# A graph-network layer on one core: the W2 sum leaves GpSimd, and two matmul rounds take up what is no longer summed

## What is computed

```python
xs, xv = _split(x, 64, 32)          # of node_features[col], col = dst
es, ev = _split(e, 8, 8)
s1 = einsum('ea,eb,abc->ec', xs, es, W1) * c1
s2 = einsum('eai,ebi,abc->ec', xv, ev, W2) * c2
out_s = (s1 + s2) * inv_sqrt2
v1 = einsum('ea,ebi,abc->eci', xs, ev, W3) * c3
v2 = einsum('eai,eb,abc->eci', xv, es, W4) * c4
out_v = (v1 + v2) * inv_sqrt2
messages = concatenate([out_s, out_v]) @ Wm + bm
agg = segment_sum(messages, row)    # row = src
upd = concatenate([node_features, agg]) @ Wu + bu
out = layernorm(x + node_features + upd)
```

## Time and profile before

| | |
|---|---|
| median of 3 runs | 2093.25 us (2091.78 to 2100.47) |
| the profiled execution | 2112.58 us |
| its span | 2110.8 us |
| TensorE matmul busy | 1648.6 us, 78% of the span |
| VectorE busy | 1647.6 us, 78% |
| GpSimd busy | 1333.6 us, 63% |
| ScalarE busy | 911.8 us, 43% |
| TensorE clock granted, mean | 0.916 |

### The profile page before, as it was taken

How to read it: one execution, slowest core, us unless ns; L and a number is a source line. 1 busy time by engine, 2 the same in 40 slices (tenths; PEclk the granted TensorE clock), 3 DMA queues, 4 the chain that set the end, 5 groups by cost and what they waited for, 6 DMA issues and landing times.

```text
span 2110.8 us, 37127 instructions
## 1 busy us (share of the span) xinstructions
PE 1648.6 (78%) x11180; PEld 987.9 (47%) x11180; DVE 1647.6 (78%) x1976; ACT 911.8 (43%) x1770; POOL 1333.6 (63%) x1082
## 2 busy tenths in 40 slices
PE   2535878787877887888787787878877878589995
PEld 1213444444444444444444444444444444388884
DVE  3545787878788788888888887878878888289996
ACT  1212444444444444444344343434443444267776
POOL 3206777777777777777777777777777777512221
PEclk9767998999999999989999999989989999899998
DMA  7996777777777777777777777777777776499996
GB/s 259 378 374 177 199 214 208 225 201 215 207 209 215 204 226 206 208 225 200 217 210 206 217 206 219 209 210 209 209 208 208 210 209 153 70 381 391 392 389 226
DMA packets 192108, 490.83 MB, mean 233 GB/s; under 512 B 51924, under 2 KB 104212, under 8 KB 166994
## 3 DMA queue, kind: packets, MB, share of 16 engines
q1 hardware_dynamic: 108994, 381.38, 51.6%
q0 software_dynamic: 83088, 109.13, 24.5%
HBM read 393.52 MB, written 96.88 MB: 232 GB/s over the span
## 4 chain that ended last, share of the span: by engine, by line
issue 23%; POOL 20%; DMA 18%; PE 16%; DVE 11%; ACT 3%; another core or an unknown queue 3%; SPq 2%; DVEq 1%; POOLq 1%; ACTq 0%
DMA agg<-summed,row_idx 13%; POOL agg L330 9%; POOL xg L305 7%; POOL prod L315 5%; DVE prod L521 4%; DMA agg<-start_rows 4%; PE ps L665 4%; PE ps L660 3%; PE ps L717 2%; DVE stats L609 2%; PE ps L648 2%; ACT prod L465 2%; PE ps L718 1%; PE ps L719 1%
## 5 line engine op out<-in xcount | busy, mean ns | idle before, releaser
L665 PE MATMUL ps<-prod,w_sb 128*32 128x512 f32 x2352 | 624.5, 665 | 335.5 <-POOL prod L315 246.3
L330 POOL DMA_INDIRECT agg<-summed,row_idx x392 | 623.8, 1591 | 399.9 <-DMA agg<-summed,row_idx 245.9
L521 DVE TENSOR_TENSOR prod<-ps,e_sb 128x2048 f32<-128x2048 f32 x294 | 662.4, 2285 | 187.3 <-PE ps L648 125.6
L305 POOL DMA_INDIRECT xg<-in_x_rows,dst_sb x392 | 399.3, 1019 | 146.3 <-issue 101.9
L315 POOL TENSOR_TENSOR prod<-prod 128x512 f32<-128x512 f32 x196 | 360.7, 1840 | 18.0 <-DVE prod L521 18.0
L529 DVE TENSOR_TENSOR prod<-ps,e_sb 128x3072 f32<-128x3072 f32 x98 | 328.0, 3347 | 0.2 <-PE ps L656 0.2
L509 DVE TENSOR_TENSOR prod<-ps,e_sb 128x2048 f32<-128x2048 f32 x98 | 223.9, 2285 | 102.8 <-PE ps L665 65.4
L432 ACT ACTIVATE summed<-ps 128x644 f32<-128x644 f32 x98 | 69.3, 707 | 541.2 <-PE ps L720 460.3
L665 PEld LDWEIGHTS ps<-prod,w_sb 128*32 128x32 f32 x2352 | 105.9, 112 | 378.9 <-POOL prod L315 267.3
L660 PE MATMUL ps<-prod,w_sb 128*32 128x512 f32 x1176 | 214.4, 617 | 0.0
L762 PE MATMUL ps<-wux_a,prod 128*128 128x160 f32 x784 | 181.0, 313 | 30.8 <-DVE prod L591 27.2
(11 more groups left out here) (62 smaller groups left out, 2358.1 us busy)
## 6 DMA issues: line engine op xcount, KB each, us to landing
e_sb<-in_e_rep SPq DMA_DIRECT2D x98, 1536.0 KB
e_sb<-in_e_rep SPq DMA_DIRECT2D x98, 1024.0 KB
agg<-start_rows SPq DMA_DIRECT2D x50, 640.0 KB, 5.1
prod<-in_x_t SPq DMA_DIRECT2D x98, 320.0 KB, 5.8
prod<-agg SPq DMA_DIRECT2D x97, 320.0 KB, 5.5
out<-prod POOLq DMA_DIRECT2D x97, 320.0 KB, 5.4
row_sb<-in_src_row SPq DMA_DIRECT2D x98, 256.0 KB
xg<-in_x_rows,dst_sb POOLq DMA_INDIRECT x392
```

Source lines behind the costliest of these rows:

```text
L305: nc.gpsimd.indirect_dma_start(xg[g[1] % 2][:, q, :], None, x_rows, bass.IndirectOffsetOnAxis(dst_sb[g[1]][:, q:q + 1].bitcast(U32), 0)).t ...
L330: nc.gpsimd.indirect_dma_start(agg, bass.IndirectOffsetOnAxis(row_idx[g[1]][:, q:q + 1].bitcast(U32), 0), summed[g[1]][:, q // 2, q % 2 * ...
L521: nc.vector.tensor_tensor(prod[g[1] % 2][:, 4 + 4 * i:8 + 4 * i, :].rearrange("p (a b) e -> p a b e", b=2), ps[:, t_bank(g, 1 + i), :].uns ...
L665: return nc.tensor.matmul(ps[32 * quarter:32 * quarter + 32, S_BANK, :], w[:, 32 * half:32 * half + 32], prod[g[1] % 2][:, tile, :], start ...
```

## The change

GpSimd's adds go away. VectorE makes one add of 1024 columns in place of two of 512: tiles 6 and 7 receive 10 and 11, after `times_xv(g, 1)`. Tiles 14 and 15 are no longer added to anything, and W2 contracts them itself: the scalar rounds take eight tiles (0 to 3, 6, 7, 14, 15). A new function `round_rest` follows `round_y` with four matmuls: one in quarter 0, one in quarter 1 and two in quarter 3. The count of rounds for a group is eight. GpSimd's slot becomes two gathers, two scatters, two gathers, two scatters. VectorE makes both steps of `rows` ahead of `times_xv(s, 0)`. TensorE transposes the first third of the next group's vectors after `round_w2`, no longer at the slot's end.

```diff
@@ -20,7 +20,7 @@
 ET = 10
 NPROD = 22
 USES = 6
-ROUNDS = 6
+ROUNDS = 8
 XW = 224
 MW = D + 1
 SET_ROWS = 8
@@ -307,14 +306,6 @@
                     bass.IndirectOffsetOnAxis(dst_sb[g[1]][:, q:q + 1].bitcast(U32), 0)
                 ).then_inc(x_gathered[g[1]], 16)
 
-            def add_parts(g, step):
-                pool.wait_ge(multiplied, number(g) * USES + 3 + step)
-                if step:
-                    pool.wait_ge(parts_added_pool, number(g) * 2 + 1)
-                total = prod[g[1] % 2][:, 6, :]
-                nc.gpsimd.tensor_tensor(total, total, prod[g[1] % 2][:, 10 + 4 * step, :],
-                                        ALU.add).then_inc(parts_added_pool, 1)
-
             def scatter(g, q):
                 if q == 0:
                     pool.wait_ge(summed_copied, number(g) + 1)
@@ -333,19 +324,13 @@
 
             def slot(s):
                 live = lambda d: not isinstance(s[0], int) or 0 <= number(s) + d < n_groups
-                for q in range(TILES):
+                for pair in range(2):
                     if live(2):
-                        gather(shift(s, 2), q)
-                if live(-3):
-                    scatter(shift(s, -3), 0)
-                    scatter(shift(s, -3), 1)
-                if live(0):
-                    add_parts(s, 0)
-                if live(-3):
-                    scatter(shift(s, -3), 2)
-                    scatter(shift(s, -3), 3)
-                if live(0):
-                    add_parts(s, 1)
+                        gather(shift(s, 2), 2 * pair)
+                        gather(shift(s, 2), 2 * pair + 1)
+                    if live(-3):
+                        scatter(shift(s, -3), 2 * pair)
+                        scatter(shift(s, -3), 2 * pair + 1)
 
             run_slots(pool, slot, -2, n_groups + 3, 8, (n_groups - 2) // M1 * M1)
@@ -531,13 +516,10 @@
                                         e_sb[g[1] % 2][:, 4:ET, :].rearrange("p (i f) e -> p f i e", f=2),
                                         ALU.mult).then_inc(multiplied, 2)
 
-            def add_parts(g, step):
-                dve.wait_ge(multiplied, number(g) * USES + 3 + step)
-                if step:
-                    dve.wait_ge(parts_added_dve, number(g) * 2 + 1)
-                total = prod[g[1] % 2][:, 7, :]
-                nc.vector.tensor_tensor(total, total, prod[g[1] % 2][:, 11 + 4 * step, :],
-                                        ALU.add).then_inc(parts_added_dve, 1)
+            def add_parts(g):
+                dve.wait_ge(multiplied, number(g) * USES + 3)
+                total = prod[g[1] % 2][:, 6:8, :]
+                nc.vector.tensor_tensor(total, total, prod[g[1] % 2][:, 10:12, :], ALU.add).then_inc(parts_added, 1)
 
             def rows(g, step):
                 n = number(g)
@@ -566,16 +548,13 @@
                     times_xs(s)
                 if live(-3):
                     rows(shift(s, -3), 0)
+                    rows(shift(s, -3), 1)
                 if live(0):
                     times_xv(s, 0)
-                if live(-3):
-                    rows(shift(s, -3), 1)
-                if live(0):
                     times_xv(s, 1)
+                    add_parts(s)
                     times_xv(s, 2)
-                    add_parts(s, 0)
                     times_y(s)
-                    add_parts(s, 1)
 
             run_slots(dve, slot, 0, n_groups + 3, 8, n_groups // M1 * M1)
@@ -661,7 +640,9 @@
                                         start=start, stop=stop)
 
             def scalars(g, quarter, k, half, start=False, stop=False):
-                tile, w = (k, w1_sb[:, k, :]) if k < 4 else (6 + k - 4, w2_sb[:, k - 4, :])
+
+                tile = (0, 1, 2, 3, 6, 7, 14, 15)[k]
+                w = w1_sb[:, k, :] if k < 4 else w2_sb[:, k % 2, :]
                 return nc.tensor.matmul(ps[32 * quarter:32 * quarter + 32, S_BANK, :], w[:, 32 * half:32 * half + 32],
                                         prod[g[1] % 2][:, tile, :], start=start, stop=stop)
@@ -683,10 +664,9 @@
                 scalars(g, 3, 1 + f, 0).then_inc(rounds, 1)
 
             def round_w2(g):
-                pe.wait_ge(parts_added_pool, number(g) * 2 + 2)
-                pe.wait_ge(parts_added_dve, number(g) * 2 + 2)
+                pe.wait_ge(parts_added, number(g) + 1)
                 for quarter in range(3):
-                    scalars(g, quarter, 3 + quarter, 1, stop=True)
+                    scalars(g, quarter, 3 + quarter, 1, stop=quarter == 2)
                 scalars(g, 3, 3, 0).then_inc(rounds, 1)
 
             def round_y(g, f):
@@ -694,7 +674,13 @@
                     pe.wait_ge(multiplied, number(g) * USES + 6)
                 for i in range(3):
                     vectors(g, i, 16 + 3 * f + i, sum_sb[:, :], stop=f == 1)
-                scalars(g, 3, 4 + f, 0, stop=f == 1).then_inc(rounds, 1)
+                scalars(g, 3, 4 + f, 0).then_inc(rounds, 1)
+
+            def round_rest(g):
+                scalars(g, 0, 6, 1, stop=True)
+                scalars(g, 1, 7, 1, stop=True)
+                scalars(g, 3, 6, 0).then_inc(rounds, 1)
+                scalars(g, 3, 7, 0, stop=True).then_inc(rounds, 1)
 
             def messages(g):
                 pe.wait_ge(S_copied, number(g) + 1)
@@ -740,13 +726,14 @@
                     transpose_xs(after)
                 if live(-1):
                     round_w2(before)
+                if live(1):
+                    transpose_xv(after, 0)
                 if live(-2):
                     sum_same(two_before)
                 if live(-1):
                     round_y(before, 0)
                     round_y(before, 1)
-                if live(1):
-                    transpose_xv(after, 0)
+                    round_rest(before)
 
             run_slots(pe, slot, -1, n_groups + 2, 8, (n_groups - 1) // M1 * M1)
```

More of the change, by code:

```diff
@@ L157, in build @@
         nodes_out = [sem(f"nodes_out{b}") for b in range(M2)]
-        parts_added_pool = sem("parts_added_pool")
         pool_passed = sem("pool_passed")
@@ L185, in build @@
         multiplied = sem("multiplied")
-        parts_added_dve = sem("parts_added_dve")
+        parts_added = sem("parts_added")
         idx_step = sem("idx_step")
```

## The result

The changed kernel takes **1966.97 us** (median of 4 runs, 1963.45 to 1973.67), the kernel before 2096.86 beside it (4 runs). The ratio is **0.937**, with a 95% interval of 0.9339 to 0.9401. I had predicted 2016 us and a range of 1890 to 2130, so the time lies within the range, and the gain is 130 us where I forecast 77. The profile shows that this is right for a reason that is partly wrong. All ratios count the executions within 1.5% of a kernel's fastest alone, which matters most for the changed kernel with late transposes, where it leaves out two of four executions and later four of six.

The account below looks back on a forecast made before the run. GpSimd's chain of 17.35 us was taken to bound the 17.50 us slot. TensorE's loop of 14.90 plus 1.80 of hold gives 16.7: 74 us over 92 slots, plus 5, less 2, off 2093 is 2016 us, range 1890 to 2130.

Parts of the forecast that it names:

- 5.14: GpSimd's wait in us from second to third scatter, including landing; used for both waits, giving a 14.1 us slot.
- GpSimd stays the bound: Rival: two open landing waits, each grown from 5.14 to 6.8 us, slot 17.5, 2090 us; chance 0.10.
- The moved gathers: GpSimd's third and fourth gathers, 2.7 us, go into the first landing wait: 4.6 us against 5.14.
- 14.90 us plus the hold: TensorE's loop from S copy to S copy after the change, claimed to set the slot.
- the hold: Time from the end of TensorE's last round's record to the S copy; taken as 1.80 us, cause unknown.
- Paid in full, 1.77: TensorE's round_rest: four more steps, 1.77 us, claimed to lie wholly on the path that sets the slot.
- My first rival: No hold: 0.07 us left, slot 15.0 us, 1860 us in all; chance 0.24.
- 16.7 forecast: Main case's slot in us: TensorE's loop of 14.90 plus 1.80 of hold, 0.8 less than before; chance 0.46.
- the slot with 4.08: A slot of the kernel before with edge loads, where the hold lasted 4.08 us, until the scatter pair ended.
- forecast 1.21: VectorE's single add of 1024 columns, claimed to take 1.21 us.
- 13.6 us of own work: VectorE's own work in a slot after the change, below TensorE's loop.
- forecast 5 and 2: 5 us gained before the sixth group's times_xs; 2 us lost at the end to the last group's extra rounds.

Follow-up runs that it names:

- changed kernel with late transposes: Changed kernel, TensorE's transposes for times_xv 0 put back to the end of its slot: 1910.21 us, ratio 0.8996; repeated, 1985.34 us, ratio 0.9254.
- six-round kernel with the new order: Changed kernel without round_rest, both 1024-column adds on VectorE, two gathers then two scatters, twice, on GpSimd: 1936.38 us, ratio 0.9197.
- light loads: Changed kernel with each group's second edge load cut from 1536 KB to 256 KB after the first two groups (output differs): 1850.69 us, ratio 0.8794.
- changed with the old order: Changed kernel with GpSimd put back to four gathers, then four scatters: 2113.31 us, ratio 1.0019.
- early transposes: Kernel before, with only TensorE's transposes for times_xv 0 of the next group moved ahead of sum_same: 2109.49 us, ratio 1.0022.

## Why the prediction was right and where it was wrong

**GpSimd: the step that failed.** "With 5.14 for both waits the slot is 14.1; GpSimd stops being the bound." It stayed the bound. The 5.14 was the first pair's figure, and I gave it to both pairs. The first pair's own mean in the kernel before is not far off: 5.28 over the 75 slots from 300 to 1600 us. But that mean has two parts. In 43 slots the second scatter starts 3.4 to 3.5 us after the issue of a 1536 KB load, and the next pair comes 5.95 later; in 32 it starts 6.0 to 7.9 after, and the next pair comes 4.38 later. One slot of the first kind, from GpSimd's timeline of the kernel before:

```profile
305.50 1.57 POOL L330 DMA_INDIRECT agg<-summed,row_idx  x1 [0.31 <-issue]
...
312.40 1.56 POOL L330 DMA_INDIRECT agg<-summed,row_idx  x1 [4.00 <-DMA agg<-summed,row_idx]
```

The second pair's second scatter started 2.4 to 7.1 us ahead of a load, and the pair after it came only 8.4 later, behind an add and four gathers, with no wait. So no row of the kernel before gave the landing time that the change laid open.

In the changed kernel I counted from the second scatter of a pair to the next pair, over the 164 pairs from 300 to 1600 us. The 82 whose second scatter starts from 4.5 us before to 1.5 us after the issue of a 1536 KB load take 7.0 on average, and all of them wait. The other 82, which start earlier than that before it or at least 5.0 after it, take 4.8, near the 4.5 at which there is no wait, and 6 wait. Two pairs of 1.92 and of these make 15.6 us, and the slot is 15.8. The bounds of 4.5 and 1.5 are read from this kernel and do not carry over as they stand: in the six-round kernel with the new order the same split gives 5.7 on both sides. The rival "GpSimd stays the bound" had this mechanism right, with landings ending the idle time in both pairs and no wait for row_idx. I gave it 0.10 and priced it at 6.8 for each wait; the mean is 5.9.

That the loads have a part in it is shown by the light loads (0.9 us a slot). That the pairs and the loads lock onto each other, so that moving any step of TensorE moves the waits, is argued, not shown, from the table (1.9 to 4.6 us of waits for the same eight DMAs in the kernels without adds on GpSimd) and from the spread of the late-transposes kernel. On the sharing the Trainium skill has a line: its page "DMA: Bandwidth & Descriptors", section "SWDGE vs HWDGE vs iDMA", says that software and hardware descriptors feed different queues in each DMA engine, and that the engine goes round them in turn. The longer waits beside a load agree. The same page of the Trainium skill has a fit of 2.0 us plus bytes over 436 GB/s (section "Anatomy of one DMA — SWDGE (gpsimd) path"). It gives an estimate of 2.2 us for a scatter of 80 KB. The shortest time after which a waiting pair started, in the kernel before from 300 to 1600 us, was 4.2 us, so here the measurement and the fit differ.

**The moved gathers, not the removed adds.** I had costed the moved gathers at nothing, hidden in the landing wait. That was right, and it was the main term: they stand where the wait would be bare. Of the changed kernel's 130 us the order is worth all, given the rest of the change (changed with the old order: 1.002). Alone, without the removal of the adds, it is worth 2%. The adds alone are worth 3.1%; beside two more rounds and the old order they are worth nothing. So the parts don't add up. That the order is worth less beside the adds fits with one cover (adds or gathers) being enough for one wait. Why the same four gathers and four scatters wait 3.85 us a slot with six rounds and 4.61 with eight is not shown.

**TensorE.** "14.90 us plus the hold" stands: the unhindered loop is 14.81 and the light loads show it as a floor. round_rest takes four steps, as forecast: with the last step of y ahead of it, it is one row of 2.31 us, four times 0.43 and 0.59. "Paid in full, 1.77", though, failed: only a path that sets the slot is paid for, and taking round_rest away gave 0.4.

**The hold: the other step that failed.** I took 1.80 and got 0.06. My first rival had 0.07, and so has the Trainium skill's rule of the tail (page "TensorE: Matmul & The Clock Gate", section "The cost: per-tile semaphore tail"), with which this trace agrees. The rival's time of 1860 needed GpSimd out of the way as well. My 1.8 of hold that didn't come, and the 1.0 that GpSimd's chain adds to TensorE's 14.8, made up for each other in part: 16.7 forecast, 15.8 measured. That the time came out within the range is luck to that extent. The step was wrong in another way too: the hold cost nothing before. It was time that TensorE and ScalarE had to spare behind GpSimd, as the early transposes show. And one sum in the choice of 1.80 was short: the last round ends 14.90 after the S copy, not 14.16, which leaves out the 0.74 from the S copy to w1. With 14.16 it would have ended 0.3 ahead of the first scatter, as in the slot with 4.08; with 14.90 it is 0.4 behind, as the prediction says.

**VectorE.** The 1024-column add takes 1.22 to 1.23 us in the timeline, forecast 1.21; 13.6 us of own work never set the slot.

**Start and end.** 2.4 us gained and 6.6 lost, forecast 5 and 2. The cause of the rest is open.

TensorE's clock was granted at 0.971 against 0.916, means over the span. It isn't the cause of the gain: the changed kernel with the old order had 0.966 and no gain.

## What to carry to other kernels

When an engine issues DMAs whose landing it must then wait for, count the issues that stand between a DMA and that wait: spreading the independent gathers over both waits was worth 6.5% here once GpSimd's adds were gone (2% with them), more than removing work from the engine (3.1% alone). A landing time is not a constant. Take it over many slots, split by what else is in flight, and don't give one wait's figure to another wait that other work still covers. And a gap on an engine that is not the bound (the hold) must not be carried into the sum for the kernel after.

## What the runs showed that I had not expected

- The hold: 1.67 and 1.42 us a slot in two executions of the kernel before, on average, and 0.09 to 0.10 in each kernel that differs from it in one thing: early transposes, no adds on GpSimd, or the new order of gathers. In such a slot VectorE's times_xv 0, which waits for TensorE's transposes, is late as well (the slot of the earlier trace rows: 728.05, after 4.81 us of waiting, beside the S copy's 727.98), which points to TensorE's results coming late, not to a slow ScalarE. No cause was found for it; that it needs all three together is all that is shown.
- The time from a scatter to the next pair is 7.0 us beside an edge load and 4.8 away from one, in the changed kernel, where 4.5 is the least that the issues between them allow.
- One kernel can spread over 119 us (1879 to 1998) with the same instructions. In two of its executions the slots differ by 0.8 us, of which 0.7 are waits for landings.
- Two 128x512 adds on GpSimd, 3.69 us a slot, cost 0.2 to 1.0 us of the slot where they fall into waits for landings.
